# Cross attention beside the last two attention steps, and seven feed forward units in the seam

## The reference, cut to what matters

```python
# 1 attention with slots: 16 heads, key width 64, value width 128, 64 slots, causal
q, k, v, s = x@Wq, x@Wk, x@Wv, clip(x@Ws, -32, 32)           # by heads
z = cumlogsumexp(s); p = exp(s - z); g = exp(z_before - z)   # over time
hk = hk * g + k p^T;  ok = q hk / 8;  pv = softmax(ok)       # step by step
hv = hv * g + p v^T;  o = pv hv
o = o * rsqrt(mean(o*o) + EPS) * g_norm_weight * silu(x@Wg)
x = layernorm(x + o@Wo)
# 2 cross attention of the context (512 tokens of width 256 per batch) with itself
att = softmax((ctx@xWq^T + bq) @ (ctx@xWk^T + bk)^T)
x = layernorm(x + x @ att^T)         # einsum('bln,bmn->blm', x, att): 512 x 512
# 3 feed forward, hidden width 2048, ternary weights, 8 bit activations
gate, up = quant(x) @ tern(w_gate)^T, quant(x) @ tern(w_up)^T
h = hadamard(silu(gate) * up) / sqrt(2048)
x = layernorm(x + quant(h) @ tern(w_down)^T)
```

## Time and profile before

| | us |
|---|---|
| median of 3 runs | 1675.48 |
| lowest, highest | 1673.68, 1675.9 |
| profiled execution, time | 1672.5 |
| profiled execution, span | 1670.7 |
| TensorE busy | 1539.9 (92%) |
| VectorE busy | 1048.4 (63%) |
| ScalarE busy | 634.7 (38%) |
| GpSimd busy | 389.9 (23%) |
| mean granted clock of TensorE | 0.982 of full speed |

### The profile page before, as it was taken

The page is one execution under the profiler, slowest core; times in us unless marked ns, Lnnn a source line. Parts: engine busy times, 40 slices in busy tenths (PEclk is TensorE's granted clock), DMA queues, the critical chain, the costliest instruction groups (busy, mean ns, idle before and its releaser), DMA issues.

```text
span 1670.7 us, 23953 instructions
## 1 busy us (share of the span) xinstructions
PE 1539.9 (92%) x9534; PEld 1209.0 (72%) x9570; DVE 1048.4 (63%) x1982; ACT 634.7 (38%) x1215; POOL 389.9 (23%) x270
## 2 busy tenths in 40 slices
PE   7999999999999999999999999999778787898986
PEld 5887888788788877878888877888655455565664
DVE  4555556655555566566555665665776767677775
ACT  4332333223223322233233332332325465637663
POOL 1111002001100112333333433242013323223210
PEclk9999999999999999999999999999989998999998
DMA  7111101111101100111211112110401133232551
GB/s 257 35 57 38 30 28 64 38 39 42 54 26 32 51 26 32 45 57 38 64 64 46 51 47 74 39 51 13 170 14 38 57 109 104 72 95 90 157 158 57
DMA packets 86527, 106.99 MB, mean 64 GB/s; under 512 B 4497, under 2 KB 58897, under 8 KB 86033
## 3 DMA queue, kind: packets, MB, share of 16 engines
q1 hardware_dynamic: 84496, 99.17, 18.6%
q0 software_dynamic: 1920, 6.29, 0.9%
HBM read 78.19 MB, written 27.26 MB: 63 GB/s over the span
## 4 chain that ended last, share of the span: by engine, by line
PE 59%; DVE 19%; issue 12%; POOL 5%; ACT 3%; DMA 2%; SPq 0%; DVEq 0%; POOLq 0%; ACTq 0%
PE bank L361 12%; PE bank L363 11%; PE bank L362 11%; PE bank L572 4%; DVE OG L978 4%; PE bank L470 3%; POOL sm L1254 3%; PE bank L607 3%; DVE sm L969 2%; DVE ZT L917 2%; DVE AM L925 2%; PE bank L456 2%; PE bank L432 2%; PE bank L427 2%; PE bank L478 2%
## 5 line engine op out<-in xcount | busy, mean ns | idle before, releaser
L361 PE MATMUL bank<-Wh,XTh 128*128 128x512 f32 x512 | 211.5, 413 | 0.0
L363 PE MATMUL bank<-Wh,XTl 128*128 128x512 f32 x512 | 200.8, 392 | 0.0
L362 PE MATMUL bank<-Wl,XTh 128*128 128x512 f32 x512 | 199.9, 390 | 0.0
L691 ACT ACTIVATE V<-bank 128x256 f32<-128x256 f32 x128 | 49.2, 385 | 373.1 <-PE bank L363 373.1
L1254 POOL TENSOR_TENSOR sm<-sm,half 128x8 f32<-128x8 f32 x32 | 52.8, 1651 | 528.1 <-DVE sm L972 528.1
L361 PE MATMUL bank<-XTh,Wh 128*128 128x512 f32 x384 | 160.9, 419 | 12.4 <-DVE XTl L867 12.4
L363 PE MATMUL bank<-XTh,Wl 128*128 128x512 f32 x384 | 151.1, 393 | 0.0
L362 PE MATMUL bank<-XTl,Wh 128*128 128x512 f32 x384 | 150.2, 391 | 0.0
L907 DVE SCALAR_TENSOR_TENSOR U<-U,bank 128x256 f32<-128x256 f32 x128 | 53.7, 419 | 148.4 <-ACT U L693 148.4
L572 PE MATMUL bank<-XT,W 128*128 128x512 bf16 x484 | 122.8, 396 | 25.8 <-DVE M L1121 8.6
L995 DVE TENSOR_TENSOR Y<-Y,bank 128x512 f32<-128x512 f32 x128 | 87.8, 688 | 69.9 <-PE bank L363 69.9
(11 more groups left out here) (189 smaller groups left out, 3250.3 us busy)
## 6 DMA issues: line engine op xcount, KB each, us to landing
z_scratch<-EV SPq DMA_DIRECT2D x64, 256.0 KB, 2.1
Z<-z_scratch SPq DMA_DIRECT2D x16, 1024.0 KB, 5.9
RAW<-wgT SPq DMA_DIRECT2D x16, 512.0 KB, 3.8
RAW<-wuT SPq DMA_DIRECT2D x16, 512.0 KB, 3.7
RAW<-wdT SPq DMA_DIRECT2D x16, 512.0 KB, 3.6
w_scratch<-BW POOLq DMA_DIRECT2D x24, 256.0 KB, 4.3
W<-w_scratch SPq DMA_DIRECT2D x3, 2048.0 KB, 14.1
RAW<-Wo SPq DMA_DIRECT2D x8, 512.0 KB, 3.8
```

The costliest lines, as they stand in the source:

```text
L361: engine.matmul(o, lh(c), rh(c), start=c == 0, stop=False)
L362: engine.matmul(o, lh(c), rl(c), start=False, stop=False)
L363: last = engine.matmul(o, ll(c), rh(c), start=False, stop=c == n - 1)
```

## The change

The orders are rewritten. `beside_place(b, places)` yields the next place of batch b each time it is called; in loop n = 30 it is called 14 times, once after nearly every stage. ctx, centre and n1 of batch 0 come at the end of loop 29. The seam holds the last two places of batch 0, all 16 of batch 1, and units 0 to 6; the feed forward loop begins with unit 7 and has batch 2 beside units 7 to 22 and batch 3 beside 23 to 38.

```diff
 def attention_order():
     for n in range(STEPS - 1):
+        beside = iter(range(14) if n == STEPS - 2 else ())
         yield "keys", n
         yield "q", n + 1
+        yield from beside_place(0, beside)
         yield "scores", n
         yield "states", n
+        yield from beside_place(0, beside)
...
         yield "vg3", n + 1
+        yield from beside_place(0, beside)
         if n and n % 4 != 2:
             yield "tern", next(tern, None)
+        if n == STEPS - 3:
+            for stage in ("ctx", "centre", "n1"):
+                yield stage, 0
+
+def beside_place(b, places):
+    for j in places:
+        return cross_place(b, j)
+    return ()
 
 def seam_order():
+    n = STEPS - 1
+    for item in (("keys", n), (0, 14), ("scores", n), ("states", n), (0, 15), (1, 0), ("turn_o", n - 1), (1, 1), ("ok", n),
+                 (1, 2), ("y", n - 1), (1, 3), ("turn_ok", n), (1, 4), (1, 5), ("turn_w", n), (1, 6), (1, 7),
+                 ("weights", n), (1, 8), ("unit", 0), ("values", n), (1, 9), ("unit", 1), (1, 10), ("unit", 2),
+                 ("turn_o", n), ("leave_o", 0), (1, 11), ("unit", 3), ("y", n), ("leave_y", 0), (1, 12), ("unit", 4),
+                 (1, 13), ("unit", 5), (1, 14), ("unit", 6), (1, 15)):
...
+def cross_place(b, j):
+    for stage in BESIDE[j]:
+        yield stage, b
+    if j >= 14 and b + 1 < NB:
+        for stage in ("ctx", "centre") if j == 14 else ("n1",):
+            yield stage, b + 1
+
+SEAM_UNITS = 7
+LAG = 23
+
+def ffn_place(n):
+    # the body of the former ffn_order loop, with
+    b, j = divmod(n - SEAM_UNITS, 16)
+    if 0 <= b < 2:
+        yield from cross_place(b + 2, j)
+
 def ffn_order():
+    for n in range(SEAM_UNITS, 60 + LAG + 13):
+        yield from ffn_place(n)
```

```diff
-        XTh = sb("XTh", [128, 4, TOK], R, A)
-        XTl = sb("XTl", [128, 4, TOK], R, A)
+        X = sb("X", [128, NB, 2, 4, T], R, A)
...
+        XT, SB = (XT0, XT1, XT2), (SB0, SB1, SB2)
```

The first feed forward matmuls wait for the loads of gate and up weights separately, down for its own. The evacuation of x_turned may run one batch further ahead, and for batch 1 waits for attention step 30:

```diff
-                    act.wait_ge(S["up"], 16 * b - 16)
-                    engine.activation(XT[:, b % 2, 0:2, :],
+                    act.wait_ge(S["up"], 16 * (b - 2))
+                    if b == 1:
+                        act.wait_ge(S["ov_sum"], 2 * (STEPS - 1))
+                        act.wait_ge(S["o_gated"], STEPS - 1)
+                    engine.activation(XT[b % 3][:, 0:2, :],
```

ScalarE now issues the ternary stores, each ahead of the next tile's rounding; GpSimd no longer does:

```diff
+            def store(j):
+                act.wait_ge(S["w3_made"], j + 1)
+                engine.dma_start(scratch[j // 8][:, 1024 * (j % 8):1024 * (j % 8) + 1024], BW[:]).then_inc(S["w3_store"], 16)
...
+                if t is None:
+                    store(23)
+                elif what == "made" and j:
+                    store(j - 1)
```

The copies of IDB and H128 move from the seam to ScalarE's start of the attention phase. ScalarE's and VectorE's first ctx waits for the projections of step 30. SP's order of loads changes:

```diff
+            engine.dma_start(XB[:, 0:1], xbq.rearrange("(p a) -> p a", a=1)).then_inc(S["xb_in"], 16)
+            engine.dma_start(XB[:, 1:2], xbk.rearrange("(p a) -> p a", a=1)).then_inc(S["xb_in"], 16)
...
             for no, (key, where) in enumerate(pieces):
+                if no == len(pieces) - 6:
+                    sp.wait_ge(S["proj_vg"], 4 * (STEPS - 3))
+                    engine.dma_start(XW[:, 0], xWqT.rearrange("(c p) n -> p c n", p=128)).then_inc(S["xw_in"], 16)
+                    engine.dma_start(XW[:, 1], xWkT.rearrange("(c p) n -> p c n", p=128)).then_inc(S["xw_in"], 16)
+                    context(0)
...
+            sp.wait_ge(S["xq_made"], 2)
+            context(1)
             sp.wait_ge(S["proj_vg"], 4 * STEPS)
-            sp.wait_ge(S["x_lo_g"], 4)
             sp.wait_ge(S["w_lo_g"], 42)
             sp.wait_ge(S["w3_made"], 24)
             sp.wait_ge(S["w3_store"], 16 * 24)
+            for k in range(3):
+                engine.dma_start(W3[:, k, :], scratch[k]).then_inc(S[f"w3_in{k}"], 16)
```

More of the change, by code:

```diff
@@ new lines, in beside_place @@
+def beside_place(b, places):
+    for j in places:
+        return cross_place(b, j)
+    return ()
+def seam_order():
+    n = STEPS - 1
[4 more added lines that the diff above has]
+                 (1, 13), ("unit", 5), (1, 14), ("unit", 6), (1, 15)):
+        if item[0] == "unit":
+            yield from ffn_place(item[1])
+        elif item[0] in (0, 1):
+            yield from cross_place(*item)
+        else:
+            yield item
@@ L91 @@
         ("turn_q", 8), ("down", 10))
-def ffn_order():
-    lag = 23
-    for stage in ("ctx", "centre", "n1"):
-        yield stage, 1
-    for n in range(60 + lag + 13):
-        b, j = divmod(n, 16)
-        for stage, unit in (("gate", n), ("h", n - 1), ("gs", n), ("high", n - 2), ("low", n - 3), ("had2", n - lag),
-                            ("had1", n - 4), ("had1_out", n - 5), ("had2_out", n - lag - 1), ("absmax", n - lag - 2)):
-            if 0 <= unit < 64:
-                yield stage, unit
-        i, rest = divmod(n - 20, 4)
-        if rest == 0 and 0 <= i < 16:
-            yield "read", i
-        for stage, off in TILE:
-            i, rest = divmod(n - lag - off, 4)
-            if rest == 0 and 0 <= i < 16:
-                yield stage, i
-        if b < 3:
-            for stage in BESIDE[j]:
-                yield stage, b + 1
-        if j >= 14 and b < 2:
-            for stage in ("ctx", "centre") if j == 14 else ("n1",):
-                yield stage, b + 2
-        if n < 64:
-            yield "silu", n
+SEAM_UNITS = 7
+LAG = 23
+def ffn_place(n):
+    for stage, unit in (("gate", n), ("h", n - 1), ("gs", n), ("high", n - 2), ("low", n - 3), ("had2", n - LAG),
+                        ("had1", n - 4), ("had1_out", n - 5), ("had2_out", n - LAG - 1), ("absmax", n - LAG - 2)):
+        if 0 <= unit < 64:
+            yield stage, unit
+    i, rest = divmod(n - 20, 4)
+    if rest == 0 and 0 <= i < 16:
+        yield "read", i
+    for stage, off in TILE:
+        i, rest = divmod(n - LAG - off, 4)
+        if rest == 0 and 0 <= i < 16:
+            yield stage, i
+    b, j = divmod(n - SEAM_UNITS, 16)
+    if 0 <= b < 2:
+        yield from cross_place(b + 2, j)
+    if n < 64:
+        yield "silu", n
+def ffn_order():
+    for n in range(SEAM_UNITS, 60 + LAG + 13):
+        yield from ffn_place(n)
+FEED = {"gate", "h", "gs", "silu", "high", "low", "had1", "had1_out", "had2", "had2_out", "absmax", "read", "turn_q", "down",
+        *(stage for stage, _ in TILE)}
 def raw_tasks():
@@ L219, in build @@
         A.close()
-        W3 = sb("W3", [128, 3, 8192], BF)
         XI = sb("XI", [128, 4, 512])
@@ L568, in ffn @@
                     pe.wait_ge(S["xt_evac1"], b + 1)
-                    pe.wait_ge(S["w3_in"], 48)
-                    for w, bk, done in ((WG, bg, S["gate"]), (WU, bu, S["up"])):
+                    for k, w, bk, done in ((0, WG, bg, S["gate"]), (1, WU, bu, S["up"])):
+                        pe.wait_ge(S[f"w3_in{k}"], 16)
                         for c in range(4):
-                            mm = engine.matmul(bk[:], w[:, c, 128 * j:128 * j + 128], XT[:, b % 2, c, :],
+                            mm = engine.matmul(bk[:], w[:, c, 128 * j:128 * j + 128], XT[b % 3][:, c, :],
                                                start=c == 0, stop=c == 3)
```

192 lines of the change are left out of this document (95 added, 97 removed).

## The result

The changed kernel takes 1685.6 us (median of 4 runs, 1684.5 to 1688.7) against 1675.35 for the kernel before: ratio 1.0066, 95% interval 1.0048 to 1.0083. The forecast was 1670.5 and a gain of 5; the result is a loss of 10. The profiled execution has a span of 1682.7 us.

The account below looks back on a forecast made before the run. TensorE bounds the attention loop, VectorE's in-order queue the seam. Terms -8.7 (order), +0.9 (bias loads) and +2.8 (SP's hold) sum to -5.0, giving 1670.5 us; 8-in-10 range 1652 to 1686, the forecast's own 1664.5 to 1676.5.

Parts of the forecast that it names:

- The wait of SP: Step 28: SP holds a raw tile and issues three other loads first, so states start late; +2.8 us, between 0 and 6.
- -8.7: Rearranged order as a whole: unit 7 starts 46.3 us later than unit 0 did, the units after save 55.0.
- the walk: The prediction's pass through VectorE's in-order queue, adding work and waits for stretch 1 and stretch 2, then the units.
- 23.4 and 14.7: Waits in us that the prediction listed along VectorE's queue for stretch 1 and stretch 2, beside work of 55.1 and 69.1.
- stretch 2: From the last x_made of batch 0 to unit 7's gate product: 83.8 us, VectorE's share above 80%.
- stretch 1: From 1140.27 to the last x_made of batch 0: VectorE's work 55.1 plus waits 23.4, ending at 1218.8.
- the seam is VectorE's, and there they add their full 8.7 us: Seven units in the seam: VectorE bounds it, so their two products each (7 x 1.25) win little.
- Units 7 to 22 are what units 0 to 15 are now: 74.25: Units beside batch 2 would take the 74.25 us that units 0 to 15 take in the kernel before.
- TensorE's wait before x_turned: End of stretch 1: TensorE, done with vg3 near 1206, idles some 12 us for x_made of batch 0.
- The coupling costs more: slower: Rival, stretch 1 and stretch 2: VectorE's share falls to 72%, 172.5 us, +10.2, time 1680.7; chance 0.25.
- unit 7 would be wrong beyond 1315: Sign for the profile after: unit 7's gate product near 1306; prediction wrong if before 1295 or after 1315.
- The clock: Rival: matmuls after stalls run at half rate, about 1.4 us each; stretch 2 grows 5.6, time 1676; chance 0.08.

Follow-up runs that it names:

- e7: Changed kernel with SP's hold two pieces from the end instead of six and the first read of Z behind the context load of batch 3: 1676.0 us.
- e16: The same kernel as e8, run again: 1673.4 us, ratio 0.9984 to 1.0002 to the kernel before.
- e8: Changed kernel with the old order of all stages and SP's hold two pieces from the end instead of six: 1671.6 us.
- e11: e7 with turn_o and y of step 30 moved earlier and the first three places of batch 0 in loop 30 behind k and ok: 1674.6 us.
- e13: e8 with ctx, centre and n1 of batch 0 moved from the seam into loop 30 before VectorE's waits, and qk ahead of scores: 1668.7 us.
- e15: e11 with centre and n1 of batch 0 inside loop 29 where VectorE waits, instead of at its end: 1670.7 us.
- e17: e13 with qk of batch 0 put back behind turn_o of step 30: 1664.0 us, ratio 0.9942 to the kernel before.
- e5: Changed kernel without the reciprocal of z in step 31 (3.35 us of VectorE): 1686.4 us, three runs.
- e3: Changed kernel without units in the seam; units 0 to 15 beside batch 2, 16 to 31 beside batch 3: 1683.8 us.
- e2: Changed kernel with the first read of the z scratch issued after the context load of batch 3 instead of before it: 1683.6 us.
- e9: Kernel before with the 24 ternary stores issued by ScalarE instead of GpSimd: 1674.6 us.
- e6: Changed kernel without the pass with X1l in the x_m product of batch 1 (3.7 us of TensorE): 1691.0 us, two runs.
- e14: Changed kernel with the edits of e5 and e6 at once: 1685.7 us, two runs.

## Why the prediction was wrong

The direction failed. 1685.6 still lies inside the wide range of 1652 to 1686, at its upper end, and outside the forecast's own of 1664.5 to 1676.5.

**The wait of SP, mis-sized.** "Ends: 0 ... and 6 ...; I take 2.8" was the right chain at the wrong size: 6.8 us in the trace, 5.4 to 9.8 by medians. The failed number is the landing "after the 3.6 us that such a piece takes", which is the median over the run; with the engines 0.86 busy it took 6.8. The rule of the Trainium skill, DMA: Bandwidth & Descriptors, Rules for kernel authors, pointed the right way. The estimate by that page's fixed cost and bandwidth, 4.9 us from the end of the hold, was short too: the piece was used 8.4 us after the first of the four issues (1067.05 to 1075.49). The page gives these figures for transfers that GpSimd issues, and this one is SP's.

**"-8.7" for the part, wrong in sign.** With both mis-sized loads mended the new order is 2.6 to 4.4 us slower than the old one (e7 against e16 and e8), where the walk had 8.7 faster. The step that failed is the list of waits: 23.4 and 14.7 were put together along VectorE's queue for two stretches that never ran before, and came out 27.8 and 21.8. (The items listed for the first add to 23.6, and those of "+13.7" for units 23 to 38 to 13.5; neither matters here.) VectorE's work was right. I followed one engine and took the waits of the others as known. The list lacks k behind qk's bank (5.3) and the context and its roots at the end of stretch 2. These two are seen in the trace, but their price is not shown: e11 took the first away and unit 7 moved 0.6 us.

Part of the gap is where ctx, centre and n1 of batch 0 stand. The walk took their work (7.9 us in the expectation of e13) as part of stretch 1; e15 shows that waits of loop 29 can take part of it, with 4.0 us less by the median. With such pieces well placed in both orders, the new one (e15, 1670.7) is still 6.6 us behind the old one (e17, 1664.0).

**"the seam is VectorE's, and there they add their full 8.7 us".** In the old seam the first half holds: work moved out of VectorE's part (e13, e17) moved its end, by more than 1 to 1 once the bank wait was gone (7.6 us less work, 9.4 us shorter). In stretch 2 of the new order it does not: 3.35 us less of VectorE gave 1.6 (e5). The second half held: without the seven units the seam was 10 us shorter (e3), for the 8.7 of the walk.

**"Units 7 to 22 are what units 0 to 15 are now: 74.25".** Wrong by 7.2. VectorE's work in them is the same (54.7 us of VectorE, 54.3 before), but they begin with a full pipeline of units, and SP's read of Z meets the context of batch 3. Without units ahead of them (e3) the first three steps take 9.8 us, between the 11.4 of after and the 8.2 of before, so the pipeline is about half of those 3.2 us; the rest is not explained. e2 shows the 4.4 of the other place (4.0 of them went), though its median fell by 2.0 only. I counted SP's instructions that move with the edit, but not which other transfer each now falls beside.

**Right.** VectorE's work, TensorE's wait before x_turned (7.9 and 4.2 for "some 12"), the pattern of units 23 on (within 3% for the two stretches), the stores on ScalarE at nothing (e9), the biases near nothing. The rival "The coupling costs more: slower" is what happened, with its share of 72% and its 172.5 us (175.5 measured, beyond its deciding point of 167.3), if not with its price alone, as SP's wait came on top. Of the statements on the profile after, that unit 7 would be wrong beyond 1315 caught it (1323.2); VectorE's share in stretch 2 was 76%, not above 80%, TensorE waited 6.1 us for Et instead of "3 to 4", and TensorE did end over half of VectorE's waits in stretch 2, which the prediction had named as a sign that it is wrong. The granted clock was 0.88 and 0.90 in the two stretches, near the 0.87 of the old seam; no run here parts the share of the rival "The clock" from the waits that bring it.

**Luck.** From unit 7 to the end the kernel took 359.5 us, and the walk had 359.3 (275.5 and the drain of 83.85). This is +7.2 in units 7 to 22 against -7.0 in the rest.

**Open.** Why removing work in e5, e6 and e14 did not lower the medians, how the 2.6 to 4.4 us between e7 and e8 divide among the fourteen places, and what a really filled gap before x_turned would give.

## What to carry to other kernels

Before work is interleaved with a loop, look for the waits of the engine that has to do it, and put each piece in front of one that is as long as the piece: 6.8 us of VectorE went into loop 30 for nothing in this way, while the same stages at the end of loop 29 pushed a reciprocal, and the whole chain behind it, by 8 us. For every bank of PSUM that an added stage takes, ask behind which instruction of its reader it comes free. A load moved ahead of another costs the second one more than its issue (here 3 us more to landing, with the DMA engines 0.86 busy): take the landing time under load.

## What was not expected of the hardware

- A 512 KB load that in the median landed in 3.6 us took 6.8 behind about 0.8 MB of others and beside a second of its kind.
- The issue of a store of 256 KB took SP 3.59 us directly behind a read of 1 MB; the median of the 64 such stores is 0.32.
- Matmuls put behind a wait of 6.5 us came at half speed: in e11 the y product started 0.43 us apart for its first 5.7 us, and the stretch that holds it had a clock of 0.76 instead of 0.89.
